# Score maxima of a gated cross-attention: one 308-column matmul on the whole TensorE array, or four 32-row tiles of 78 columns

## The reference

```python
q = proj(_layernorm(x), Wq, bq)      # 16 heads of 32
k = proj(ctx, Wk, bk); v = proj(ctx, Wv, bv)
scores = einsum('bhqd,bhkd->bhqk', q, k) / sqrt(32)
attn = softmax(scores, axis=-1)      # over 77 keys
x = x + tanh(g_xattn) * (einsum('bhqk,bhkd->bhqd', attn, v) @ Wo.T + bo)
x = x + tanh(g_ffn) * ffn(_layernorm(x))
```

## Time and profile before

| | |
|---|---|
| median of 3 runs | 642.86 us (641.58 to 643.01) |
| profiled execution | 640.81 us, of which the span of the trace is 639.0 us |
| TensorE busy | 576.6 us, 90% of the span |
| VectorE busy | 482.9 us, 76% |
| ScalarE busy | 335.1 us, 52% |
| GpSimd busy | 189.8 us, 30% |

### The profile page before, as it was taken

One profiled execution on the slowest core, in us unless ns is written; L12 is line 12 of the kernel. 1 busy time (PEld: TensorE's weight loads), 2 busy tenths in 40 slices (PEclk: granted clock), 3 DMA queues, 4 the chain that ended last, 5 costly groups with the idle time before them and its releaser, 6 DMA issues. The chain is left out here.

```text
span 639.0 us, 9653 instructions
## 1 busy us (share of the span) xinstructions
PE 576.6 (90%) x3259; PEld 326.3 (51%) x3283; DVE 482.9 (76%) x695; ACT 335.1 (52%) x408; POOL 189.8 (30%) x160
## 2 busy tenths in 40 slices
PE   3979689999998999999989755999999969999997
PEld 3744435756656567575575442444444424444443
DVE  6768965988869878789576785789999688964441
ACT  3245167263562633725517236977776768554440
POOL 4016245251242321522303130000000909803562
PEclk9999979999999999999999995999999989999999
DMA  8921000530010100101001117677776969889753
GB/s 306 391 89 67 0 2 10 194 129 0 8 57 0 69 0 1 67 1 66 1 0 67 64 69 279 246 280 290 275 278 241 424 239 358 314 319 353 263 197 131
DMA packets 37185, 98.15 MB, mean 154 GB/s; under 512 B 2720, under 2 KB 3488, under 8 KB 32544
## 3 DMA queue, kind: packets, MB, share of 16 engines
q1 hardware_dynamic: 37152, 97.72, 40.7%
HBM read 55.77 MB, written 41.94 MB: 153 GB/s over the span
## 5 line engine op out<-in xcount | busy, mean ns | idle before, releaser
L1154 PE MATMUL ps<-h_sb,w_q 128*128 128x512 bf16 (+1 forms) x500 | 115.4, 382 | 3.3 <-ACT h_sb L1183 1.7
L1406 PE MATMUL ps<-w_q,h_q 128*128 128x512 bf16 x438 | 96.3, 380 | 0.5
L1154 PEld LDWEIGHTS ps<-h_sb,w_q 128*128 128x128 bf16 x512 | 49.2, 98 | 58.5 <-issue 4.4
L993 POOL TENSOR_TENSOR c_lo<-c_sb,c_hi 128x512 fp32r<-128x512 f32 x32 | 41.2, 1300 | 127.1 <-ACT c_hi L569 127.1
L1486 POOL TENSOR_TENSOR xo<-xo,b2s 128x512 f32<-128x512 f32 x32 | 56.4, 1794 | 60.1 <-DMA xo<-x_dram 41.8
L1406 PEld LDWEIGHTS ps<-w_q,h_q 128*128 128x128 bf16 x448 | 43.8, 98 | 52.9
L604 ACT ACTIVATE q_hi<-ps,bq_sb 128x512 fp32r<-128x512 f32 x32 | 22.0, 688 | 92.8 <-PE ps L338 92.8
L1198 ACT ACTIVATE xo<-ps,b1s,sc 128x1024 f32<-128x1024 f32 x48 | 57.9, 1205 | 18.7 <-PE ps L1154 17.3
L1270 DVE TENSOR_REDUCE hmax<-xo 128x1024 f32 (+1 forms) x48 | 57.2, 1213 | 11.4 <-ACT xo L1198 11.4
L556 ACT ACTIVATE prob<-ps 77x1024 f32<-77x1024 f32 x64 | 61.6, 1012 | 5.9 <-PE ps L380 5.9
L1002 POOL TENSOR_TENSOR x<-x,bo_gate 128x512 f32<-128x512 f32 (+1 forms) x32 | 43.2, 1362 | 48.4 <-DVE xn L723 32.7
(11 more groups left out here) (136 smaller groups left out, 1066.6 us busy)
## 6 DMA issues: line engine op xcount, KB each, us to landing
h_dram<-xo SPq DMA_DIRECT2D x48, 512.0 KB, 2.7
h_sb<-h_dram SPq DMA_DIRECT2D x16, 1024.0 KB, 11.2
x_dram<-x SPq DMA_DIRECT2D x8, 1024.0 KB, 3.9
xo<-x_dram SPq DMA_DIRECT2D x8, 1024.0 KB, 4.8
x<-h_dram SPq DMA_DIRECT2D x8, 1024.0 KB, 8.0
x<-in_x SPq DMA_DIRECT2D x7, 1024.0 KB, 5.4
out<-xo SPq DMA_DIRECT2D x7, 1024.0 KB, 4.5
x<-in_w_t SPq DMA_DIRECT2D x1, 4096.0 KB, 17.2
```

The source lines that it names most:

```text
L993: nc.gpsimd.tensor_tensor(c_lo[:, g, :], c_sb[:, g, :], c_hi[:, g, :].bitcast(F32), ALU.subtract).then_inc(c_lo_on, 1)
L1154: mm = nc.tensor.matmul(ps[:, 2 * (m % 2) + s, :], w1_q[:, k, m * P:(m + 1) * P], xq_t[:, one(2 * j + s), k, :], start=(k == 0), stop=(k = ...
L1406: mm = nc.tensor.matmul(ps[:, 4 * s + t, :], h_q[:, s, m, t * P:(t + 1) * P], w2_q[:, m, :], start=(m == 0), stop=(m == MF - 1))
```

## The change

`k_hi` is no longer block-diagonal: it has the layout of `k_lo`, [128, 4 groups, 77 keys], with one more column for each group, which is kept at zero (78 columns, `NKE`). `scores_by_token` issues 16 matmuls in place of four: for each t, four matmuls of 32 rows, 128 weight columns and 78 moving columns, head r on row group r of the array and into bank r at column 78 t. VectorE's maximum reads the same number of values in the order (t, r, key) through another access pattern. The semaphore of the call is raised by two matmuls, those of the last t for r = 1 and r = 3, where the last matmul raised it once. `split_k` becomes one ScalarE and one VectorE instruction. POOL's fill shrinks to the four spare columns, and the wait for it moves from ScalarE to TensorE's first score call.

```diff
-            sh.k_hi = sb("k_hi", [P, HEADS, NK], F32R)
+            sh.k_hi = sb("k_hi", [P, GROUPS, NKE], F32R)
...
                     for t in range(TT):
-                        mm = nc.tensor.matmul(ps[:, t, 0:4 * NK], q_hi[:, m, t * P:(t + 1) * P],
-                                              k_hi[:, 4 * m:4 * m + 4, :].rearrange("p h n -> p (h n)"),
-                                              start=True, stop=True)
-                    mm.then_inc(smax_mm, 1)
+                        for r in range(4):
+                            rows = slice(DK * r, DK * (r + 1))
+                            mm = nc.tensor.matmul(ps[:, r, t * NKE:(t + 1) * NKE], q_hi[rows, m, t * P:(t + 1) * P],
+                                                  k_hi[rows, m, :], start=True, stop=True)
+                            if t == TT - 1 and r % 2:
+                                mm.then_inc(smax_mm, 1)
...
-                    for r in range(4):
-                        hi = k_hi[DK * r:DK * (r + 1), :, :].rearrange("p (g r) n -> p g r n", r=4)[:, :, r, :]
-                        nc.scalar.copy(hi, sh.k_t[DK * r:DK * (r + 1), :, b * NK:(b + 1) * NK]).then_inc(k_split_hi, 1)
+                    nc.scalar.copy(k_hi[:, :, 0:NK], sh.k_t[:, :, b * NK:(b + 1) * NK]).then_inc(k_split_hi, 1)
...
-                    for r in range(4):
-                        dve.wait_ge(k_split_hi, 4 * b + r + 1)
-                        q = slice(DK * r, DK * (r + 1))
-                        hi = k_hi[q, :, :].bitcast(F32).rearrange("p (g r) n -> p g r n", r=4)[:, :, r, :]
-                        last = nc.vector.tensor_tensor(k_lo[q, :, :], sh.k_t[q, :, b * NK:(b + 1) * NK], hi, ALU.subtract)
-                    last.then_inc(k_split, 1)
+                    dve.wait_ge(k_split_hi, b + 1)
+                    nc.vector.tensor_tensor(k_lo[:, :, :], sh.k_t[:, :, b * NK:(b + 1) * NK], k_hi[:, :, 0:NK].bitcast(F32),
+                                            ALU.subtract).then_inc(k_split, 1)
...
-                    dve.wait_ge(smax_mm, KD * c + m + 1)
+                    dve.wait_ge(smax_mm, 2 * (KD * c + m) + 2)
...
-                                            ps[:, 0:TT, 0:4 * NK].rearrange("p t (h n) -> p t h n", n=NK),
+                                            ps[:, 0:4, 0:TT * NKE].rearrange("p r (t n) -> p t r n", n=NKE)[:, :, :, 0:NK],
...
-                nc.gpsimd.memset(k_hi[:, :, :].bitcast(F32), 0.0).then_inc(k_zeroed, 1)
+                nc.gpsimd.memset(k_hi[:, :, NK:NKE].bitcast(F32), 0.0).then_inc(k_zeroed, 1)
```

More of the change, by code:

```diff
@@ L31 @@
 NK = 77
+NKE = NK + 1
 F = 2048
@@ L342, in scores_by_token @@
                 def scores_by_token(c, m):
+                    if is_step(c, 0) and m == 0:
+                        pe.wait_ge(k_zeroed, 1)
                     pe.wait_ge(q_hi_on, KD * c + m + 1)
@@ L373, in scores_by_key @@
                             rows = slice(DK * r, DK * (r + 1))
-                            nc.tensor.matmul(ps[0:NK, r, :], k[rows, g if k is k_lo else 4 * g + r, :], q[rows, g, :],
+                            nc.tensor.matmul(ps[0:NK, r, :], k[rows, g, 0:NK], q[rows, g, :],
                                              start=(k is k_hi and q is q_hi), stop=False)
@@ L539, in split_k @@
                         act.wait_ge(k_biased, GROUPS)
-                        act.wait_ge(k_zeroed, 1)
-                    for r in range(4):
-                        hi = k_hi[DK * r:DK * (r + 1), :, :].rearrange("p (g r) n -> p g r n", r=4)[:, :, r, :]
-                        nc.scalar.copy(hi, sh.k_t[DK * r:DK * (r + 1), :, b * NK:(b + 1) * NK]).then_inc(k_split_hi, 1)
+                    nc.scalar.copy(k_hi[:, :, 0:NK], sh.k_t[:, :, b * NK:(b + 1) * NK]).then_inc(k_split_hi, 1)
                 def xt_high(c, t):
```

## The result

| | before | after |
|---|---|---|
| median | 642.22 us (641.49 to 643.01, 4 runs) | 648.16 us (647.23 to 650.30, 4 runs) |
| profiled execution, its span | 640.81, 639.0 us | 647.23, 645.4 us |
| end of the last output projection | 378.1 us | 384.2 us |
| granted TensorE clock over the span | 0.973 | 0.963 |

The changed kernel is slower, ratio 1.0097 (95% interval 1.0065 to 1.0129). The time lies in the range, but it is 5 us above the forecast, and far outside the 1.3 us that I called no change. All of it arises in attention: the last output projection ends 6.1 us later, and what follows takes 260.9 us before and 261.2 after.

The account below looks back on a forecast made before the run. TensorE, busy for 90% of the span, and its waits were taken as the bound. Step terms 0.38 - 0.2 + 0.7 + 0.38 - 0.8 gave +0.5 us: 641.3 profiled, 643.3 median, range 640.0 to 650.0.

Parts of the forecast that it names:

- the price of a tile call: Score call on TensorE, from end of one stream to start of the next: 0.76 us against 0.57, 0.19 longer.
- Rivals 1 and 2: Score calls: instruction starts set the pace, 657 us profiled, chance 0.10; row groups don't load side by side, 684, chance 0.04.
- rival 3: Score calls: loads don't bind, sets follow at 0.035 us; about -6 us in all, 635 profiled, chance 0.07.
- the wait for `xt_lo`: TensorE's wait after call 3's maximum, 0.34 us on average, shrinks by 0.2 in each of five steps.
- the release of VectorE: End of a score call: VectorE released 0.2 us earlier at call 3 (0.64, not 0.84), unchanged at call 2 (0.73).
- step 4 without its clock stretch: Key split as single instructions frees VectorE 1.44 us earlier, removing the wait before call 1; -0.8 us for step 4.
- rival 4: VectorE's reduction pays for a new bank every 77 values; at 0.15 us more, +2.4, 643.7 profiled, chance 0.13.
- rival 5: VectorE's multiply precedes POOL's work, the whole `xt_lo` wait goes, tiling changes cost less; about -2.2 us, 639.1 profiled, chance 0.08.
- what would show it: Signs in the profile after, among them 0.65 us from calls 0 and 1's first load record to the next projection's first matmul.
- The sum of +0.5 us: Attention steps: 0.38 - 0.2 + 0.7 + 0.38 - 0.8 = +0.5 us, giving 641.3 profiled, 643.3 median.
- Where this counts in a step: Score calls 0 and 1 cost 0.19 us each, call 2 nothing, call 3 at most 0.03 either way.
- rival 1: Score calls limited by how fast instructions start, 0.029 us each; 657 us profiled, 659 median, chance 0.10.

Follow-up runs that it names:

- f_one_tile: Kernel before, plus one tile matmul of 32 rows and 8 columns in the middle of score calls 0 and 1; 645.94 us, ratio 1.0069.
- k_wide: Changed kernel, but each score tile streams 234 columns in place of 78, only the first 78 kept; 646.07 us, ratio 1.0070 to the kernel before.
- h_tiles_23: Both key layouts kept: score calls 2 and 3 use the tiles, calls 0 and 1 the whole array; 646.76 us, ratio 1.0077 to the kernel before.
- c_fill_after: Changed kernel, first four of twelve output projection matmuls moved into the wait before score call 3, steps 2 to 7; 643.23 us, ratio 1.0024 to kernel before.
- a_four_pieces: Changed kernel with the keys split in four pieces again on ScalarE and VectorE; 647.68 us, ratio 1.0090 to the kernel before.
- g: Both key layouts kept: score calls 0 and 1 use the tiles, calls 2 and 3 the whole array; 644.59 us, ratio 1.0051 to the kernel before.
- b: Kernel before, each score matmul streaming 78 of 308 columns except the first call of all streams, output not the reference's; 638.37 us, ratio 0.9950.
- i: Kernel before, plus one tile matmul of 32 rows and 8 columns in the middle of score calls 2 and 3; 652.00 us, ratio 1.0173.
- d: Kernel before, first four of twelve output projection matmuls moved into the wait before score call 3, steps 2 to 7; 640.31 us, ratio 0.9981.

## Why the prediction was right or wrong

**Right: the price of a tile call.** 0.78 measured against 0.76, with 0.10 of nothing and 0.11 of bare load each way; calls 0 and 1 cost about 0.21 each, 0.19 predicted. f_one_tile measured a way in and out alone at 0.39 (0.40). Rivals 1 and 2 did not occur (16 loads and 16 matmuls pass in 0.64), nor rival 3: the pace is the load's, as k_wide shows. The Trainium skill ("TensorE: Matmul & The Clock Gate", section "Wait — 56ns, not 53.3ns?") has a floor of about 62 ns for a matmul with hardware decode off. By an estimate from it the 16 would take 0.99 us; this trace has 0.64, so the floor did not bind here. The Trainium skill ("TensorEngine Tiling (Array Packing)", section "Overview") gives a speedup of up to 4x for a dimension of 32 or less. It did not come in this trace: columns fell to a quarter, the call rose from 0.57 to 0.78.

**Right in the main: where it counts.** Calls 2 and 3 cost next to nothing by themselves: h_tiles_23 has 0.03 a step, after what the wait for `xt_lo` gives back. Mis-sized was the release of VectorE: a tile's record is 0.28 long (median of 512), so 0.24 passes after its columns, where I had taken 0.16 over from the 308-column matmul. So VectorE gained 0.12 and not 0.20 at call 3, and lost 0.05 at call 2 (0.82 from the end of the columns ahead instead of 0.77). The wait for `xt_lo` gave back 0.15 in steps 2, 3 and 5 (0.2 predicted), step 4 without its clock stretch is 0.7 to 0.8 shorter (41.63 in c_fill_after, which has none there, against 42.34; 0.8 predicted), and the wait came back as 0.54, with 0.66 in the length of the step, in a_four_pieces. The reduction still takes 1.44, so rival 4 did not occur; nor did rival 5, since the wait for `xt_lo` stayed at 0.2. One number of "what would show it" was wrong in its wording: 0.65 is near what holds from the end of the columns ahead (0.67); from the first record it is 0.57.

**Wrong: the sum, since it had no term for the clock.** The step that failed is "Where this counts in a step" with calls 2 and 3 at nothing: true of their length, but it took the speed of the matmuls behind them as given. The sum of +0.5 us became about +0.9 of direct prices and some 5 us of clock: 1.55 us for the stretch in step 4, about 1.2 in step 6, about 2.4 in step 1. No rival was put on the clock. So it is luck that the time lies in the range: its upper part was meant for a mild form of rival 1, which did not occur. Between the last query projection and the output projection before, two calls of four matmuls with 308 columns lay, and from step 2 on the clock held. With two calls of 16 tiles with 78 columns, four side by side, it does not in every step.

What is shown, for the dips from step 2 on and by one profile of each kernel: tiles in calls 2 and 3 bring them, tiles in calls 0 and 1 don't (h, g); with work in the wait or more columns in the same tiles they are not there (c, k). One such dip stands in a kernel without tiles, b. Extra ways in and out at the same calls lower the clock in the mean though all columns are there (i). Not shown: how fewer columns and empty time are connected. Open: why a dip comes in some steps and not in others, which differs from run to run; and what lengthens the stretches of steps 0 and 1. The nine profiles with any tile in the score calls, be it the single one of f or i, have 13.7 to 20.5 us at half the clock there, and the three without (before, b, d) 6.8 to 10.2. Wide tiles did not remove this, and the filling does not reach these steps.

## What to carry to other kernels

Before tiling small matmuls, count the loads and the two changes of tiling: 16 tiles of 78 columns replaced four matmuls of 308 and took longer, since each set waits for a load of 128 weight columns. Look at what TensorE does around its waits, and at the granted clock behind them: here taking out work that looked like waste was followed by half the clock, and was paid in the matmuls behind it (1.55 us in step 4). Filling a wait of TensorE is worth only what the engine that it waits for lets through; here, in steps 2 to 6, VectorE took it all back.

## What the runs showed of the hardware

- Streaming 234 columns instead of 78 through each 32-row tile lengthens a call by 0.08 us (0.65 against 0.57, k_wide), and its profile has no dips behind calls 2 and 3.
- One 8-column tile between two matmuls of the whole array costs 0.39 us (f_one_tile, call 0 to call 1: 3.75 against 3.36).
- In step 4, 2.32 of 3.40 us busy in 39 matmul records stood ahead of half the clock in the changed kernel, and 2.21 of 3.40 in 15 records ahead of the full clock in the kernel before. In steps 2, 3 and 5 the same calls of the changed kernel were not followed by half the clock.
- A stretch of 3.4 us at half the clock over the output projection behind call 3 cost 1.55 us up to the transposes of the maxima (step 4 of the changed kernel). Of the whole step about 1.2 were left in step 6.
- VectorE's reduction of 1232 values takes 1.44 us whether its runs of 77 values stay in a bank or change it each time.
